# Passage to the third layer: moments of twelve pairs, two pairs normalised ahead, odd moments on ScalarE in the first layer, zeros on TensorE at the start

## The reference

```python
h = jnp.maximum(_layernorm(x), 0.0); x = x + L0(h, adj)   # relations q k^T, masked, divided by their row norm, times v
h = jnp.maximum(_layernorm(x), 0.0); x = x + L1(h, adj)   # graph attention: leaky relu, mask, softmax, elu
h = jnp.maximum(_layernorm(x), 0.0); x = x + L2(h, adj)   # graph convolution: norm_adj @ (h @ weight) + bias
h = jnp.maximum(_layernorm(x), 0.0); x = x + L3(h, adj)   # masked multi-head attention, 8 heads of 32
def _layernorm(x, eps=1e-05):
    m = jnp.mean(x, axis=-1, keepdims=True); v = jnp.var(x, axis=-1, keepdims=True)
    return (x - m) / jnp.sqrt(v + eps)
```

## Time and profile before

| | us |
|---|---|
| median of 3 runs | 716.94 (715.76 to 717.35) |
| the profiled execution's own time | 716.58 |
| its span, first to last instruction | 714.8 |
| TensorE busy (matmul) | 692.3, 97% |
| VectorE busy | 627.9, 88% |
| ScalarE busy | 555.9, 78% |
| GpSimd busy | 462.1, 65% |

### The profile page before, as it was taken

The page is one execution under the profiler, slowest core; times in us unless marked ns, Lnnn a source line. Parts: engine busy times, 40 slices in busy tenths (PEclk is TensorE's granted clock), DMA queues, the critical chain, the costliest instruction groups (busy, mean ns, idle before and its releaser), DMA issues.

```text
span 714.8 us, 22548 instructions
## 1 busy us (share of the span) xinstructions
PE 692.3 (97%) x6938; PEld 652.9 (91%) x6938; DVE 627.9 (88%) x2618; ACT 555.9 (78%) x1892; POOL 462.1 (65%) x585
## 2 busy tenths in 40 slices
PE   5999999999999999999998999999999999999996
PEld 5999999999888888889997999999999999999994
DVE  5899888987799999699998999998889998899876
ACT  3665656565689999876665998889888988898895
POOL 2445454554587788588884776776677666766662
DMA  8222310000000000000000000000000000000001
GB/s 246 83 82 89 89 43 0 0 0 2 0 1 2 1 2 1 2 1 0 0 0 1 17 33 17 30 29 30 15 30 29 30 15 30 30 29 16 32 32 45
DMA packets 21710, 20.30 MB, mean 28 GB/s; under 512 B 2449, under 2 KB 21649, under 8 KB 21649
## 3 DMA queue, kind: packets, MB, share of 16 engines
q1 hardware_dynamic: 19456, 18.16, 8.0%
q10 hardware_dynamic: 2192, 1.44, 0.7%
HBM read 11.21 MB, written 8.39 MB: 27 GB/s over the span
## 4 chain that ended last, share of the span: by engine, by line
PE 89%; DVE 3%; ACT 3%; issue 2%; POOL 1%; DMA 1%; POOLq 0%; ACTq 0%; DVEq 0%
PE bank L397 43%; PE bank L1276 8%; PE bank L387 7%; PE bank L166 5%; PE bank L1262 5%; PE bank L1286 4%; PE bank L480 4%; PE bank L837 3%; PE bank L427 3%; PE bank L377 3%; PE bank L461 1%; PE bank L875 1%; PE bank L850 1%; ACT prob L1372 1%; DMA wk<-in_L_gnn_Wk_dram 1%
## 5 line engine op out<-in xcount | busy, mean ns | idle before, releaser
L1372 ACT ACTIVATE prob<-wide,small 128x128 f32<-128x128 f32 x504 | 195.5, 395 | 2.1 <-DVE small L1484 2.1
L1447 POOL TENSOR_TENSOR prob<-prob,small 128x512 f32<-128x512 f32 x127 | 132.3, 1043 | 100.1 <-DVE small L1498 98.1
L1484 DVE CUSTOM_DVE_ANT_0 wide<-bank,mbias 128x128 f32<-128x128 f32 x512 | 115.3, 286 | 0.1
L1372 ACT ACTIVATION_READ_ACCUMULATOR prob<-wide,small 128x1 f32 x504 | 97.2, 193 | 0.0
L155 POOL TENSOR_TENSOR rstd<-vare,mhalf 128x2 f32<-128x2 f32 x104 | 73.3, 704 | 20.5 <-DVE vare L144 20.2
L1276 PE MATMUL bank<-ident,prob 128*128 128x128 f32 x512 | 72.2, 273 | 3.8 <-POOL prob L1447 3.5
L636 POOL TENSOR_TENSOR rnorm<-norm,mhalf 128x2 f32<-128x2 f32 x32 | 22.3, 696 | 81.3 <-ACT relsq L577 81.3
L129 DVE BATCH_NORM_STATS2 stats<-xs 128x6 f32<-128x256 f32 (+1 forms) x176 | 65.6, 415 | 5.9 <-DMA xs<-in_x_dram 5.0
L239 POOL TENSOR_SCALAR xn<-xs,nmean,rstd 128x256 f32<-128x256 f32 x120 | 65.3, 554 | 5.5 <-POOL rstd L155 5.5
L1392 ACT COPY probT<-bank 128x512 f32<-128x512 f32 x96 | 52.3, 580 | 18.7 <-PE bank L1276 18.7
L1276 PEld LDWEIGHTS bank<-ident,prob 128*128 128x128 f32 x512 | 58.3, 140 | 5.5 <-POOL prob L1447 4.8
(11 more groups left out here) (168 smaller groups left out, 1933.1 us busy)
## 6 DMA issues: line engine op xcount, KB each, us to landing
out_dram<-xs SPq DMA_DIRECT2D x31, 256.0 KB, 2.1
xs<-in_x_dram SPq DMA_DIRECT2D x29, 256.0 KB, 2.7
xs<-in_x_dram ACTq DMA_DIRECT2D x1, 512.0 KB, 7.8
xs<-in_x_dram ACTq DMA_DIRECT2D x1, 256.0 KB, 4.3
wq<-in_L_gnn_Wq_dram SPq DMA_DIRECT2D x1, 256.0 KB, 3.9
wk<-in_L_gnn_Wk_dram ACTq DMA_DIRECT2D x1, 256.0 KB, 5.2
wv<-in_L_gnn_Wv_dram SPq DMA_DIRECT2D x1, 256.0 KB, 5.8
w<-in_L_gnn_W_dram SPq DMA_DIRECT2D x1, 256.0 KB, 7.4
```

Of the source, the lines that this page charges most:

```text
L1372: ins = nc.scalar.activation(prob[:, r, i, :], wide[:, r, i, :], ACT.Exp, bias=nmax[r][:, i:i + 1], scale=-1.0, accum_out=rsum[r][:, i:i + 1])
L1447: nc.gpsimd.tensor_tensor(prob[:, r, :, :], prob[:, r, :, :], rinv[r].unsqueeze(2).to_broadcast([128, QUAD, N]), ALU.mult).then_inc(prob_r ...
L1484: nc.vector.tensor_tensor_reduce(out=wide[:, r, i, :], in0=SS[r][:, i * N:(i + 1) * N], in1=mbias[:, :], scale=-1.0, scalar=3e38, op0=ALU. ...
```

## The change

It does six things.

1. The list of VectorE starts with a `memset` of a 128 x 384 tile of zeros (`plain`, part of `wide`), and TensorE multiplies zeros six times (128 x 256) before it waits for the first weights. The result is never read.
2. `degrees()` moves on VectorE from before the low part of the weights' product to behind `normalise(1)`.
3. Moments of the odd pairs go to ScalarE: two `Identity` activations with accumulation (`sums_odd`) in odd steps of the first layer, two `Square` ones (`squares_odd`) in even steps; those of pair 31 after step 2 of the second layer. GpSimd takes their roots four pairs at a time (`root_odd`): three times in the first layer, once at step 11 of the second. VectorE's `moments_odd` goes.
4. `EARLY` is 12. The moments of pairs 0 to 11 are taken in steps 6 to 29 of the second layer, half a pair a step, their root arguments at steps 14, 22 and 30, their roots at steps 17 and 25 and after the last step.
5. Pairs 0 and 1 are normalised by ScalarE ahead, one graph each after steps 20, 23, 26 and 28, into the first layer's weight tiles `wq0` and `wk0`, from which `gather` reads.
6. The lists of ScalarE, GpSimd and VectorE for the passage from the second to the third layer are written anew, as the diff shows.

```diff
-        EARLY = 8
+        EARLY = 12
         def normalise_early(act, q):
             act.wait_ge(l2_two_shift, q // 4 + 1)
-            if q < 2:
-                act.wait_ge(l1_tr_done, PAIRS - 1 + q)
+            if q < 4:
+                act.wait_ge(l1_tr_done, PAIRS - 3 + q)
...
+        def normalise_ahead(act, q, g):
+            if g == 0:
+                act.wait_ge(l2_two_shift, 1)
+            ins = normalised(act, (wq0, wk0)[q], q, g)
+            if g == 1:
+                ins.then_inc(l2_xn_ready, 1)
...
+        def sums_odd(act, i):
+            act.wait_ge(l0_x_done, 2 * i + 2)
+            act.wait_ge(l1_odd_squares, since(i))
+            for g in range(2):
+                ins = nc.scalar.activation(odd_terms[:, g, :], x_of(2 * i + 1, g), ACT.Identity, scale=-1.0 / (16 * D),
+                                           accum_out=mean_odd[:, bass.ds(2 * i + g, 1)])
+            ins.then_inc(l1_odd_sums, 1)
+        def squares_odd(act, i):
+            act.wait_ge(l1_odd_sums, i + 1)
+            for g in range(2):
+                ins = nc.scalar.activation(odd_terms[:, g, :], x_of(2 * i + 1, g), ACT.Square, scale=1.0 / 16,
+                                           bias=mean_odd[:, bass.ds(2 * i + g, 1)], accum_out=var_odd[:, bass.ds(2 * i + g, 1)])
+            ins.then_inc(l1_odd_squares, 1)
+        def root_odd(pool, q):
+            pool.wait_ge(l1_odd_squares, 4 * q + 4)
+            part = slice(8 * q, 8 * q + 8)
+            nc.gpsimd.tensor_scalar(nmean_odd[:, part], mean_odd[:, part], 16.0, None, ALU.mult)
+            nc.gpsimd.tensor_scalar(vare_odd[:, part], var_odd[:, part], EPS, None, ALU.add).then_inc(l1_odd_args, 1)
+            pool.wait_ge(l1_odd_args, q + 1)
+            nc.gpsimd.tensor_tensor(rstd_odd[:, part], vare_odd[:, part], mhalf[:, :], ALU.pow).then_inc(l1_odd_root, 1)
...   (TensorE, start)
+                pe.wait_ge(c_plain, 1)
+                for _ in range(6):
+                    nc.tensor.matmul(OO[:, 0:D], plain[:, 0:128], plain[:, 128:128 + D], start=True, stop=True)
                 pe.wait_ge(qk_loaded, 32)
...   (ScalarE, step of the first layer)
                     squares(p - 1, 1 - b)
+                    if i is not None and b:
+                        sums_odd(act, i)
                     relu_T(p + 1, 1 - b)
+                    if i is not None and not b:
+                        squares_odd(act, i)
                     copy_v(p)
...   (VectorE, start)
+                nc.vector.memset(plain, 0.0).then_inc(c_plain, 1)
...
-                degrees()
...
                 normalise(1)
+                degrees()
...   (ScalarE, second layer)
+                AHEAD_STEPS = (20, 23, 26, 28)
                 for p in range(PAIRS - 1):
                     step(p)
-                    if p == PAIRS - 3:
-                        normalise_early(act, 0)
+                    if p == 2:
+                        sums_odd(act, PAIRS // 2 - 1)
+                        squares_odd(act, PAIRS // 2 - 1)
+                    if p in AHEAD_STEPS:
+                        half = AHEAD_STEPS.index(p)
+                        normalise_ahead(act, half // 2, half % 2)
                 copy_pT(PAIRS - 4)
                 copy_h(PAIRS - 1)
-                normalise_early(act, 1)
                 gathered_high(act, 0, 0)
                 softmax_exp(PAIRS - 2)
                 copy_pT(PAIRS - 3)
+                normalise_early(act, 2)
                 gathered_high(act, 1, 1)
-                normalise_early(act, 2)
...
                 normalise_early(act, 7)
+                for p in range(8, EARLY):
+                    gathered_high(act, p - 2, p % 2)
+                    normalise_early(act, p)
...   (GpSimd, second layer)
-                    if p in (22, 28):
-                        root_two(pool, (p - 22) // 6)
-                    if p % 2 and p + 2 < PAIRS:
-                        root_odd(pool, p + 2)
-                    elif p == 8:
+                    if p in (17, 25):
+                        root_two(pool, (p - 17) // 8)
+                    if p == 8:
                         root_even(pool, PAIRS // 8 - 1)
+                    if p == 11:
+                        root_odd(pool, PAIRS // 8 - 1)
...   (VectorE, second layer)
-                        if p % 2 == 0 and p > 0:
-                            moments_odd(dve, p // 2 + 1, 1)
-                        elif p % 2 and p + 4 < PAIRS:
-                            moments_odd(dve, p // 2 + 2, 0)
...
-                UNIT_STEPS = [*range(8, 16), *range(18, 26)]
+                UNIT_STEPS = range(6, 30)
...   (VectorE, passage)
-                gathered_low(dve, 3, 1)
-                elu(PAIRS - 4)
-                update_two(dve, 2, 0)
-                gathered_low(dve, 4, 0)
-                elu(PAIRS - 3)
+                for p in range(3, 7):
+                    elu(PAIRS - 7 + p)
+                    gathered_low(dve, p, p % 2)
+                    update_two(dve, p - 1, (p - 1) % 2)
+                dve.wait_ge(l1_x_done, EARLY + 1)
+                moments(dve, EARLY, l2_step, 0)
+                gathered_low(dve, 7, 1)
+                mean_variance(dve, EARLY, l2_step, 0)
+                update_two(dve, 6, 0)
+                gathered_low(dve, 8, 0)
+                root_argument(dve, EARLY, l2_step, l2_stats_ready, 0)
```

More of the change, by code:

```diff
@@ L274, in root_two, with normalised @@
             nc.gpsimd.tensor_tensor(shift_two[:, part], nmean_two[:, part], rstd_two[:, part], ALU.mult).then_inc(l2_two_shift, 1)
+        def normalised(act, tile, q, g):
+            return nc.scalar.activation(tile[:, g, :], x_of(q, g), ACT.Relu, bias=shift_two[:, 2 * q + g:2 * q + g + 1],
+                                        scale=rstd_two[:, 2 * q + g:2 * q + g + 1])
         def normalise_early(act, q):
             act.wait_ge(l2_two_shift, q // 4 + 1)
-            if q < 2:
-                act.wait_ge(l1_tr_done, PAIRS - 1 + q)
+            if q < 4:
+                act.wait_ge(l1_tr_done, PAIRS - 3 + q)
             else:
@@ L354, in moments_even @@
                 nc.vector.scalar_tensor_tensor(vare_even[:, part], var, EPS, var, ALU.add, ALU.max).then_inc(l1_even_stats, 1)
-        def moments_odd(dve, i, g):
-            b = i % 2
-            if g == 0 and i < 2:
-                dve.wait_ge(l0_xn_ready, PAIRS - 1 + i)
-            elif g == 0:
-                dve.wait_ge(l1_xn_ready, 2 * i - 2)
-            ins = nc.vector.bn_stats(stats[:, b, g, :], x_of(2 * i + 1, g))
-            if g == 1:
-                ins.then_inc(l1_step, 1)
-                dve.wait_ge(l1_step, 2 * i + 1)
-                for g in range(2):
-                    ins = nc.vector.bn_aggr(mv[:, b, g, :], stats[:, b, g, :])
-                ins.then_inc(l1_step, 1)
-                root_argument(dve, i, l1_step, l1_stats_ready, b)
         def gather_nodes(pe, ps, p, src, xn_ready):
@@ L604, in _, with step @@
                 copy_v(0)
-                def step(p, b):
+                def step(p, b, i=None):
                     copy_t(p)
@@ L618, in _ @@
                 with act.Fori(3, PAIRS // 2 - 1) as j:
-                    step(2 * j + 1, 1)
-                    step(2 * j + 2, 0)
+                    step(2 * j + 1, 1, j - 1)
+                    step(2 * j + 2, 0, j - 1)
                 copy_t(PAIRS - 1)
@@ L623, in _ @@
                 squares(PAIRS - 2, 0)
+                sums_odd(act, PAIRS // 2 - 2)
+                squares_odd(act, PAIRS // 2 - 2)
                 copy_v(PAIRS - 1)
@@ L1000, in _ @@
                         centre_first(pool, p + 2, tr_done, p + 1)
-                for p in range(4):
+                for p in range(3):
                     add_bias_two(pool, p)
-                add(PAIRS - 4)
-                add_bias_two(pool, 4)
-                add(PAIRS - 3)
-                add_bias_two(pool, 5)
-                add(PAIRS - 2)
-                add(PAIRS - 1)
+                root_two(pool, 2)
+                add_bias_two(pool, 3)
+                for p in range(PAIRS - 4, PAIRS):
+                    add(p)
+                    add_bias_two(pool, p - PAIRS + 8)
+                add_bias_two(pool, 8)
+                add_bias_two(pool, 9)
             @block.vector
@@ L1180, in _ @@
                     dve.wait_ge(l1_x_done, p + 4)
-                    step(p, p % 2, reused=p == EARLY - 1)
-                    if p < EARLY - 1:
-                        elu(PAIRS - EARLY + 1 + p)
+                    step(p, p % 2, norms=p > EARLY - 3, reused=p == EARLY - 1)
                 dve.wait_ge(l1_x_done, PAIRS)
```

51 lines of the change are left out of this document (25 added, 26 removed).

## The result

The changed kernel takes 712.17 us, the median of 4 runs (711.81 to 712.25); the kernel before, run beside it, took 716.35 (4 runs, 715.47 to 717.35). The ratio is 0.994, with a 95% interval from 0.9923 to 0.9957. So the change is worth 4.2 us by these runs, where 6.6 were forecast; the time lies inside the forecast's range, and the direction is as forecast. The 4.2 is rather too much: the kernel before, measured again beside the experiments (46 runs), has medians of 715.76, 715.8 and 715.98, which would make the change worth 3.6 to 3.8 us. The changed kernel was not measured again. The profiled execution took 712.21 us with a span of 710.3, against 716.58 and 714.8: 4.4 us less, 4.5 in the span.

The account below looks back on a forecast made before the run. TensorE was taken as the bound, gains lying only where its blocks stand too far apart. -1.75 + 0.6 - 1.9 + 0.4 - 1.4 - 2.15 - 0.4 = -6.6 us gave 710.4, range 707.8 to 714.2.

Parts of the forecast that it names:

- rival A: At the start, the zeros do nothing or the clock has fallen again when the weights come: -4.8, 712.1 us; chance 0.23.
- The start, -1.75: Zeros raise TensorE's clock before the weights' product, and VectorE's low part starts earlier without `degrees()`: -1.75 us.
- Step 2, +0.6: Second layer, step 2: four odd-moment activations before `copy_pT(0)` make it late for `attend(0)`: +0.6 us (0 to +1.5).
- VectorE relieved, -1.9: Second layer: odd moments leave VectorE, so the late steps return to TensorE's own 3.485 us: -1.9 us (0 to -1.93).
- Two pairs ahead, +0.4: Second layer, steps 20, 23, 26, 28: four graphs on ScalarE delay `copy_h`, TensorE seeing 0.1 each: +0.4 us (0 to +2.16).
- The last two steps, -1.4: End of the second layer: ScalarE's 1.08 us after step 29 and the root at step 28 go: -1.4 us.
- The passage to `outputs(4)`, 0: From `product(31)` until `outputs(4)`, each block of TensorE falls within 0.1 us of where it was.
- From `outputs(4)` to `outputs(7)`, -2.15: Passage to the third layer: VectorE no longer has moments of pairs 8 to 10 in its way: -2.15 us.
- Pairs 8 to 11, -0.4: Third layer: these pairs run at 2.30 us instead of 2.41 as long as there are no moments: -0.4 us.
- Rival B: ScalarE becomes the second layer's bound, halves and step 2 costing more: -3.5, 713.4 us; chance 0.13, half of it with A.
- C: The passage gives nothing because `outputs(5)` and `outputs(6)` wait for ScalarE's copies: -2.3 is lost, 712.7 us; chance 0.07.
- D: First layer, odd steps: `Identity` needs a second function table, loads on ScalarE costing 21 us: 731 us; chance 0.04.

Follow-up runs that it names:

- the start alone: The kernel before with only the zeros on TensorE and the move of `degrees()` behind the normalisation of pair 1: median 714.38 us, ratio 0.9981.
- the passage's load: The changed kernel with unread moments of three pairs added on VectorE between `outputs(4)` and `outputs(8)`: median 713.73 us, ratio 0.9967.
- the best version: Changed kernel with odd root at step 4, pair 2's bias later, odd sums after step 1, ahead halves behind `copy_pT`, `update_two` first in moment-free steps: 709.66 us.
- degrees first: The changed kernel with `degrees()` back ahead of the low part of the weights' product: median 713.1 us, ratio 0.9956.

## Why the prediction was right and where it failed

The total must not be read as support: 712.17 lies in the range, and is also rival A's 712.1, though A's mechanism is false. Against the sum of -6.6 the trace has -4.5: 2.9 us of misses, less 0.8 at the start that nobody forecast. The lower bound of the range, 707.8, has no working either; the terms named for it add up to 9.9, which is 707.0.

*The start, -1.75: right in size, by a wrong working.* The trace gives -2.51 to P0, of which 0.47 is the earlier transfer. 0.28 came inside the first layer: from its first block at line 422 to P0 it is 166.35 to 166.5 us in every changed kernel, against 166.7 in the kernel before and 167.0 with the start alone, so it belongs to the change and is unexplained. -1.76 is the start. Zeros off is +2.03, `degrees()` back +0.4. "Six zero matmuls at the slow price cost 6 x 3.78 / 8 = 2.8 us" failed: it took the instructions of the row for calls. With it went the 2.5 us of idleness on which rival A was built, at 0.23. Had I counted `x12`, its chance would have been small.

*Odd moments in the first layer, 0: right.* 0.41 and 0.50 us per activation plus 0.19 for reading, 0.40 and 0.50 from start to start, against 0.45 taken; from 52 us on `copy_v` has idle time before it in every step, 0.16 and 0.61 us in two neighbouring ones, against the earlier trace rows.

*Step 2, +0.6: right (+0.75)*, and gone in the experiment that splits it.

*VectorE relieved, -1.9: right, but GpSimd's root was mis-sized.* Its two preparations were taken at 0.2 together; they took 0.93 with the gaps, 2.6 us with the root against 1.84, and "a GpSimd that gets its input about 1 us sooner", which was to make it free, became +0.73 at step 12 (0.52 in most other traces). That is most of the shortfall in P4 to P29.

*Two pairs ahead, +0.4: a step failed.* Each graph costs 0.18, 0.7 together, and not through `copy_h` (TensorE "asks for `copy_h`'s result only two blocks later", which held), but through `copy_pT`, which stood behind the graph and which `attend` waits for. The size was off by 0.3; the place was another, and the cure follows from the place.

*The last two steps, -1.4: right (-1.26, which holds one of the halves at 0.18).*

*The passage to `outputs(4)`, 0: failed (+0.77).* "the same chain of ScalarE's copy, VectorE's low part and TensorE sets them" left out which GpSimd operation runs beside which VectorE operation. I followed each engine's list with durations measured alone.

*From `outputs(4)` to `outputs(7)`, -2.15: right (-2.08).* Of its cause, only half is shown.

*Pairs 8 to 11, -0.4: failed (-0.03).* "Pairs 8 to 11 run at 2.30 instead of 2.41 as long as there are no moments" took these four pairs to be free of moments. VectorE in the changed kernel, at the low part and the update of its first step in the third layer's list:

```profile
315.27 0.69 DVE L317 TENSOR_TENSOR yTs<-bank,yTs 128x512 fp32r<-128x512 f32 x1 [1.60 <-ACT yTs L312]
315.88 0.68 DVE L323 TENSOR_TENSOR xs<-bank,xs 128x512 f32<-128x512 f32 x1
316.48 0.74 DVE L135 BATCH_NORM_STATS2 stats<-xs 128x6 f32<-128x256 f32 x2
```

The moments are back at 316.48, before outputs(9) begins at 316.71; two of the four pairs have them. And without them outputs(9) still came late, 2.43 behind outputs(8): the update stood behind a low part that waited 1.60 for ScalarE's copy. With the update first the four take 9.34 instead of 9.54, so the order explains 0.2 of what is missing; 0.07 is the base, which was 9.57 and not 4 x 2.41; the rest is open.

*The last layer, 0: 0.53 are lost, and the place is known.* From O31 to the end it is 340.05 to 340.33 us in the changed kernel and the experiments on it where the granted clock stays at 1.00, against 339.61 and 339.65 in the kernel before, alone and with the start's edits; it is 339.76 where VectorE kept its odd load and 339.86 with the passage's load. 0.30 of it is lost at one point of VectorE's list. In the kernel before, and then in the changed one:

```profile
383.94 0.29 DVE L1484 CUSTOM_DVE_ANT_0 wide<-bank,mbias 128x128 f32<-128x128 f32 x1
384.15 0.08 DVE L1484 DVE_READ_ACCUMULATOR2_ANT small<- 128x1 f32 x1
```

```profile
378.88 0.29 DVE L1521 CUSTOM_DVE_ANT_0 wide<-bank,mbias 128x128 f32<-128x128 f32 x1
379.32 0.08 DVE L1521 DVE_READ_ACCUMULATOR2_ANT small<- 128x1 f32 x1 [0.15 <-issue]
```

The second instruction comes 0.23 us late while VectorE waits for nothing that the profile shows ("issue"), the custom instruction after it 0.30 late, and GpSimd's and TensorE's first blocks behind them 0.3 late. All ten traces of changed kernels at 340 or 341 us have this gap; the four below 340 don't have it, and two of these four are the ones that add instructions to VectorE's list ahead of this point. So it goes with what stands in the list before, and not with what the last layer does. What it is, is not shown. The other 0.2 come 0.03 to 0.04 at a time, once in every four pairs, in the changed kernel as in the versions with the added load, which lack the gap; they are open.

Rival B is gone: ScalarE has 37.43 of 40 busy and TensorE 40.00, and the halves and step 2 cost 0.7 and 0.75 where B had 2.16 and 1.9. C fell: from `outputs(4)` to `outputs(7)` 2.08 of 2.3 us came, and what was lost before `outputs(4)` was mostly GpSimd's addition and not a copy of ScalarE. D fell with the single load of a table, 1.28 us, in the whole trace.

## What to carry to other kernels

Before giving an engine work to bridge a wait, count what a row's instructions are in calls, and let the block end just as the data arrives; here a block that ended 1.85 us early was lost in five of eight executions, and one that ended late cost what it overlapped. When work moves to another engine, place it behind the copy that the bound engine wants first, in one step per piece. When a pair becomes ready sooner, ask what GpSimd then does sooner, and which VectorE operation is running at that moment. And cut both traces at the same blocks before believing a total: here the total agreed with a rival whose mechanism was false.

## What the runs showed of the hardware

- Granted clock and rate. The product took 3.78 us cold and 1.99 warm with the granted clock reading 1.00 in both traces. Zeros as operands are enough to raise it. The block of six (twelve instructions, 3.78 / 8 = 0.47 us each at half rate) lasted 4.9 us in the changed kernel and 5.5 in the best version, so the product began at 6.08 in the one and 6.60 in the other. Over the ten traces of changed kernels with six zeros the block lasted 4.36 to 5.49 us, and the product began between 5.98 and 6.08 in five of them, at 6.38 in one and at 6.56 to 6.60 in four. Five zeros were not tried.
- The clock can fall near the end. The stretch 700 to 705 us, first in the changed kernel, then in "degrees first":

```profile
700.00:705.00 5.00, 3.58 (x46) 2.96 (x48) 3.47 (x7) 2.10 (x5) 1.04 (x1) 1.00 0.07 23
```

```profile
700.00:705.00 5.00, 4.48 (x24) 4.01 (x22) 3.75 (x8) 1.81 (x6) 1.04 (x1) 0.66 0.01 3
```

  In "degrees first" it reads 0.50 over 702 to 704 us, the lower level. It follows waits of TensorE for GpSimd of 1.02 and 0.34 us and costs 1.1 us behind O31 (341.19 against 340.14); but the same waits, as long to 0.01 us, stand in the changed kernel, where the clock stays at 1.00, so they don't bring it about by themselves. By the mean granted clock (0.997 or 0.998) it happens in 8 of 46 later runs of the kernel before, and in some runs of most of the experiments, none of the changed kernel's four; it widens every comparison of four runs.
- A VectorE operation with two inputs in SBUF was held up by GpSimd's 512-column addition that had begun 0.02 us before (1.69 instead of 0.60 us for two) but not by its root of eight columns (0.60). Each was seen at one place.
- VectorE lost 0.3 us at one pair of instructions with nothing to wait for, in ten traces, and not in four whose list for VectorE differs ahead of it (the last layer, above).
